# Ranking edges into slots: each partition's edges sorted by node, one-hots over a slice of the tiles, four columns to one 16-bit operation

## What is computed

```python
h = relu(layernorm(x))                        # x: (50000, 128) f32
agg = segment_sum(edge_attr, src, 50000)      # edge_attr: (25000, 128) f32
z = silu(concat([h, agg]) @ W1 + b1) @ W2 + b2   # W1 256x256, W2 256x128
z = (z - mean(z)) * rsqrt(var(z) + 1e-5) * gamma + beta
out = x + z + h
```

## Time and profile before

| | |
|---|---|
| median of 3 runs | 728.39 us (728.29 to 728.58) |
| the profiled execution | 728.61 us |
| its span, first to last instruction | 727.0 us |
| PE busy | 702.9 us (97%) |
| DVE busy | 710.3 us (98%) |
| ACT busy | 630.5 us (87%) |
| POOL busy | 475.7 us (65%) |
| mean granted TensorE clock | 0.991 |

### The profile page before, as it was taken

One profiled execution on the slowest core, in us unless ns is written; L12 is line 12 of the kernel. 1 busy time (PEld: TensorE's weight loads), 2 busy tenths in 40 slices (PEclk: granted clock), 3 DMA queues, 4 the chain that ended last, 5 costly groups with the idle time before them and its releaser, 6 DMA issues.

```text
span 727.0 us, 15386 instructions
## 1 busy us (share of the span) xinstructions
PE 702.9 (97%) x4554; PEld 589.8 (81%) x4554; DVE 710.3 (98%) x2275; ACT 630.5 (87%) x2034; POOL 475.7 (65%) x414
## 2 busy tenths in 40 slices
PE   7999998799999999999999999999999999999993
PEld 3555554689898989889898989898989898988993
DVE  8999998999999999999999999999999999999998
ACT  7999996679898989898888989898989898989883
POOL 3000006777777787777787777787777787877850
PEclk9999999989999999999999999999999999999998
DMA  5000000214233333333333423242424242422212
GB/s 214 2 1 1 1 0 16 54 55 137 94 126 104 117 110 112 116 107 119 100 123 97 134 86 136 84 139 81 139 81 138 81 138 83 139 77 78 73 49 83
DMA packets 28265, 65.89 MB, mean 91 GB/s; under 512 B 8473, under 2 KB 10028, under 8 KB 28180
## 3 DMA queue, kind: packets, MB, share of 16 engines
q1 hardware_dynamic: 15604, 51.90, 20.2%
q0 software_dynamic: 12576, 12.99, 7.4%
HBM read 52.05 MB, written 25.60 MB: 107 GB/s over the span
## 4 chain that ended last, share of the span: by engine, by line
DVE 63%; issue 19%; PE 13%; POOL 1%; DMA 1%; DVEq 0%; ACT 0%
DVE T L1034 14%; DVE lo L1022 10%; DVE stat L824 10%; DVE R L1004 8%; DVE R L1029 7%; PE y L658 4%; PE za L653 2%; PE pre L653 2%; PE za L646 2%; PE pre L646 2%; DVE R L1051 2%; POOL G L436 1%; DVE guess_off L877 1%; DVE mdd L860 1%; DVE var L863 1%
## 5 line engine op out<-in xcount | busy, mean ns | idle before, releaser
L436 POOL DMA_INDIRECT G<-in_edge_attr_dram,slot_edge x388 | 465.4, 1200 | 119.8 <-issue 90.2
L741 PEld LDWEIGHTS y<-w2c,S 128*128 128x128 f32 (+1 forms) x1556 | 188.3, 192 | 8.0
L741 PE MATMUL y<-w2c,S 128*128 128x128 f32 (+1 forms) x1556 | 189.3, 275 | 0.0
L539 ACT ACTIVATE H<-X,shift,rstd 128x128 f32<-128x128 f32 x392 | 161.9, 489 | 2.8 <-DVE shift L882 2.8
L716 PE MATMUL pre<-hi,w1h 128*128 128x512 f32 (+1 forms) x392 | 164.0, 418 | 0.0
L717 PE MATMUL pre<-hi,w1l 128*128 128x512 f32 (+1 forms) x392 | 154.8, 395 | 0.0
L556 ACT ACTIVATE S<-pre,b1c 128x512 f32<-128x512 f32 (+1 forms) x196 | 125.5, 701 | 4.9 <-PE pre L721 4.8
L721 PE MATMUL pre<-lo,w1h 128*128 128x512 f32 (+1 forms) x392 | 123.3, 396 | 0.1
L1022 DVE TENSOR_TENSOR lo<-za,hi 128x1024 fp32r<-128x1024 f32 (+1 forms) x98 | 119.2, 1217 | 2.6 <-ACT hi L549 2.6
L824 DVE BATCH_NORM_STATS2 stat<-X 128x6 f32<-128x128 f32 x392 | 106.8, 282 | 0.1
L702 PE MATMUL za<-HOT,G 128*128 128x128 f32 (+1 forms) x784 | 104.9, 277 | 1.0 <-DMA G<-in_edge_attr_dram,slot_edge 0.9
(11 more groups left out here) (154 smaller groups left out, 1045.8 us busy)
## 6 DMA issues: line engine op xcount, KB each, us to landing
X<-in_x_dram SPq DMA_DIRECT2D x48, 512.0 KB, 3.6
out_dram<-R SPq DMA_DIRECT2D x48, 512.0 KB, 2.7
G<-in_edge_attr_dram,slot_edge POOLq DMA_INDIRECT x388, 2.6
X<-in_x_dram SPq DMA_DIRECT2D x1, 424.0 KB
out_dram<-R SPq DMA_DIRECT2D x2, 192.0 KB
w1f<-in_L_gnn_W_dram SPq DMA_DIRECT2D x1, 256.0 KB, 2.8
w2f<-in_L_gnn_W_dram SPq DMA_DIRECT2D x1, 128.0 KB, 2.6
srci<-in_src_dram SPq DMA_DIRECT2D x1, 85.8 KB
```

The source lines that it names most:

```text
L436: nc.gpsimd.indirect_dma_start(G[b.j][:, t, :], None, source, bass.IndirectOffsetOnAxis(ap=slot_edge[:, bass.ds(b.number(TILES, t), 1)], a ...
L539: done = nc.scalar.activation(H0[b.j][:, t, :], X[b.xj][:, t, :], ACT.Relu, bias=shift[b.j][:, t:t + 1], scale=rstd[b.ring(POWERS_LAG)][:, ...
L741: done = nc.tensor.matmul(places[t][0:r], S[c][:, m, t * r:(t + 1) * r], w2c[:, m, :], start=False, stop=True, skip_group_check=True)
```

## The change

Each partition's 200 edges (EC is now 200: 125 full partitions, three empty ones) are sorted by node, descending, on DVE: `largest` takes the eight largest of 200 keys (MAX), `strike` overwrites them with -1 (MATCH_REPLACE). A key is node * 256 + column + 1, exact in fp32. Since column n then holds each partition's n-th largest node, its tiles lie in a window computed from n alone (`window`, common to four columns). One-hots, ranks and table matmuls run over that window only. `hot_tile`, `is_slot` and `hot_slot` are made for four columns by one operation each, with the column as the innermost index, all operands fp16; `copy_ranks` brings the ranks to fp16. ACT takes all ranks. The words of an edge are now its column with the low part of its node's row, and its partition with the high part, so `table_words`, `edge_fields`, `slot_tables` decode them differently. The test for the slow path now sums the free slots, so that it also notices an edge outside its window. Sorting, unpacking and the slots of three groups earlier are interleaved by hand in `group_step`.

```diff
-BATCH = 7
-UNROLL = 4 * BATCH
-LAG_TABLE = 2 * BATCH
+SORTED = 8
+UNROLL = 40
+LAG_SLOT = 3
+LAG_TABLE = 4 * STREAMS
+WINDOW_SPREAD = 4.0
+WINDOW_MARGIN = 10.0
...
+    def window(n):
+
+        middle = (n + 0.5) / EC
+        reach = WINDOW_SPREAD * math.sqrt(middle * (1.0 - middle) / EC) + WINDOW_MARGIN / EC
+        first = max(0.0, 1.0 - middle - reach) * nodes
+        final = min(1.0, 1.0 - middle + reach) * (nodes - 1)
+        return slice(int(first) // BLOCK * TILES, (int(final) // BLOCK + 1) * TILES)
...
+    SORTS = [slice(0, SORTED)] + [slice(n, n + 2 * SORTED) for n in range(SORTED, EC, 2 * SORTED)]
...
-            nc.gpsimd.iota(edge_no[:], [[1, EC]], base=0, channel_multiplier=EC)
-            done = nc.gpsimd.iota(iota_tile[:], [[1, NT]], base=0, channel_multiplier=0, **small_iota)
+            nc.gpsimd.iota(column_no[:], [[1, EC]], base=1, channel_multiplier=0)
+            nc.gpsimd.iota(own_row[:], [[1, 1]], base=0, channel_multiplier=1, **small_iota)
+            done = nc.gpsimd.iota(iota_tile[:], [[1, NT], [0, STREAMS]], base=0, channel_multiplier=0, **small_iota)
...
-                nc.scalar.activation(junk_rank[:, s, :], counts[s][:, 0:NT], ACT.Relu, bias=neg_big[:],
+                nc.scalar.activation(junk_rank[:, s, width(column)], counts[s][:, tiles_near(column)], ACT.Relu,
...
-                    nc.tensor.matmul(counts[column.ring(STREAMS)][:, 0:NT], before[:],
-                                     hot_tile[:, column.ring(UNROLL), :], **add).then_inc(counted, 1)
+                    nc.tensor.matmul(counts[column.ring(STREAMS)][:, tiles_near(column)], before[:],
+                                     hot_tile[:, place(column), width(column), column.ring(STREAMS)],
+                                     **add).then_inc(counted, 1)
...
-                                     hot_slot[:, late.ring(UNROLL)].rearrange("p w r -> p (w r)"),
-                                     hot_tile[:, late.ring(UNROLL), :], **add).then_inc(slot_free, 1)
+                                     hot_slot[:, place(late), :, :, late.ring(STREAMS)].rearrange("p w r -> p (w r)"),
+                                     hot_tile[:, place(late), width(late), late.ring(STREAMS)], **add).then_inc(slot_free, 1)
...
+            def largest(n):
+
+                dve.wait_ge(sort_step, 2 * n + 1)
+                nc.vector.max(out=top[:, n * SORTED:(n + 1) * SORTED], in_=keys[:]).then_inc(sort_step, 1)
+
+            def strike(n):
+
+                dve.wait_ge(sort_step, 2 * n + 2)
+                nc.vector.match_replace(out=keys[:], in_to_replace=top[:, n * SORTED:(n + 1) * SORTED],
+                                        in_values=keys[:], imm_value=-1.0).then_inc(sort_step, 1)
...
+            def group_step(g):
+                late = g.plus(-LAG_SLOT)
+                if late.exists(GROUPS):
+                    copy_ranks(late)
+                if g.exists(GROUPS):
+                    sort_first(g)
...
+                    dve.wait_ge(slot_free, g.number(STREAMS, STREAMS))
+                    columns = slice(g.number(STREAMS), g.number(STREAMS, STREAMS))
+                    nc.vector.tensor_tensor(out=hot_tile[:, g.ring(UNROLL // STREAMS), 0:w], in0=iota_tile[:, near],
+                                            in1=tile_of[:, columns].unsqueeze(1).to_broadcast([P, w, STREAMS]),
+                                            op=ALU.is_equal).then_inc(tile_hot, 1)
+                    sort_second(g)
+                if late.exists(GROUPS):
+                    is_slot_of(late)
+                if g.exists(GROUPS):
+                    sort_third(g)
+                if late.exists(GROUPS):
+                    hot_slot_of(late)
...
+                nc.vector.tensor_tensor(out=hot_slot[:, g.ring(UNROLL // STREAMS)],
+                                        in0=is_slot[:].unsqueeze(1).to_broadcast([P, 2, CAP, STREAMS]),
+                                        in1=word[:, :, columns].unsqueeze(2).to_broadcast([P, 2, CAP, STREAMS]),
+                                        op=ALU.mult).then_inc(slot_hot, 1)
```

More of the change, by code:

```diff
@@ L110, in gnn_layer @@
     NT = NB * TILES
-    EC = -(-edges // P)
+    EC = next(n for n in range(-(-edges // P), edges + 1) if edges % n == 0 and n % SORTED == 0)
     FULL = edges // EC
-    REST = edges - FULL * EC
     FIRST_BLOCKS = 3
@@ L117, in gnn_layer, with common @@
     LAST_SMALLS = 9
[L118 to L121, removed]
+    assert FULL % 16 and 16 < FULL < P and EC < 1 << COLUMN_BITS and nodes <= OUTSIDE < 1 << 16
+    assert EC % UNROLL == 0 and UNROLL % STREAMS == 0 and NT <= 512 and SORTED % STREAMS == 0
+    def window(n):
[4 more added lines that the diff above has]
+        return slice(int(first) // BLOCK * TILES, (int(final) // BLOCK + 1) * TILES)
+    GROUPS = EC // STREAMS
+    def common(g):
+        near = [window(n) for n in range(g * STREAMS, (g + 1) * STREAMS)]
+        return slice(min(w.start for w in near), max(w.stop for w in near))
+    WINDOWS = [common(g) for g in range(GROUPS)]
+    WIDEST = max(w.stop - w.start for w in WINDOWS)
+    SORTS = [slice(0, SORTED)] + [slice(n, n + 2 * SORTED) for n in range(SORTED, EC, 2 * SORTED)]
+    assert SORTS[-1].stop == EC
     GROUP = max(n for n in range(1, 129) if edges % n == 0)
@@ L276, in run_columns, with tiles_near, width, place @@
                 step(Item(n))
[L278 to L290, removed]
+        def tiles_near(column):
+            return WINDOWS[column.group(STREAMS)]
+        def width(column):
+            return slice(0, tiles_near(column).stop - tiles_near(column).start)
+        def place(column):
+            return column.ring(UNROLL) // STREAMS
         last = Block(NB - 1)
@@ L807, in _ @@
[L807 to L817 removed]
+            dve.wait_ge(src_loaded, 16 * 2)
@@ new lines, in sort_third, with copy_ranks @@
+            def sort_third(g):
+                ahead = sort_number(g) + 1
+                if sort_number(g) == 0 and sort_place(g) == 1:
+                    strike(2 * ahead)
+                    tile_fields(SORTS[ahead], ahead)
+                    tiles(SORTS[ahead], ahead)
+                elif sort_place(g) == 2 and ahead < len(SORTS):
+                    tiles(SORTS[ahead], ahead)
+            def copy_ranks(g):
+                dve.wait_ge(ranked, g.number(STREAMS, STREAMS))
+                columns = slice(g.number(STREAMS), g.number(STREAMS, STREAMS))
+                nc.vector.tensor_copy(rank16[:, columns], rank[:, columns]).then_inc(ranks_copied, 1)
@@ L941, in _ @@
+            largest(0)
+            strike(0)
+            as_integers(SORTS[0], 0)
+            tile_fields(SORTS[0], 0)
+            tiles(SORTS[0], 0)
+            for n in range(GROUPS + LAG_SLOT):
+                group_step(Item(n))
             dve.wait_ge(counts_copied, 1)
```

275 lines of the change are left out of this document (142 added, 133 removed).

## The result

The changed kernel takes **710.71 us**, median of 4 runs (710.52 to 711.05), against 728.34 us for the kernel before in the same session (728.23 to 728.58): a ratio of 0.9757, with an interval of 0.9745 to 0.9769. The forecast was 708.6 us, range 700 to 723, faster with 0.84. The sign and the range held; the time is 2.1 us above the forecast.

What follows compares the result with a forecast made beforehand. DVE was taken to bound the front stage after the change, narrowly over PE's upper price. Tables copied 21.3 us earlier plus 1.5 us of table arithmetic gave -19.8 us: 708.6 us, range 700 to 723.

Steps and rivals of the forecast that it cites:

- What bounds after: Front stage, ranking edges into slots: DVE stays the bound at 1.61 us per group of four columns, 80.6 us for 50.
- its signs: Front stage: hot_slot near 0.42 us, 160-tile hot_tile near 0.49, MAX near 0.36, first table copy at 87 to 90 us.
- PE well under: Sign for the front stage: DVE over 95% busy and PE well under that.
- the second rival: Front stage: PE becomes the bound through weight loads or stride, +18.4 us, 727 us, about no change; chance 0.10.
- The 16-bit price: DVE's three large operations per group, 1299 elements with 16-bit operands: 0.52 ns per element, 0.68 us.
- The first rival: DVE's 16-bit operations still run at one element per cycle: 33.8 us more, 742 us, slower; chance 0.12.
- Sorting: DVE, per four groups: two MAX 0.56, two MATCH_REPLACE 0.84, nine small operations 0.81; 2.21 us, 0.55 per group.
- PE after: Front-stage matmuls over windows: three per column at 0.17 to 0.37 us, 0.67 to 1.46 us per group, not the bound.
- ACT after: Front-stage rank sums over 128 elements start every 0.25 us: 1.0 us per group, not setting the pace.
- The head: Before the first hot_tile: iota_tile takes 1.46 us (0.46 to 1.84), first hot_tile at 6.9 us, 1.3 later than 5.57.
- The end: After the last group: three steps of 0.11 us, then 0.89 us kept to the words' copy; tables copied at 88.7 us.
- Table arithmetic: Extra decoding operations: +0.4 us over the first 24 columns, +1.1 in block 1, +1.5 in all.

Runs made afterwards that it cites:

- experiment 3: Changed kernel with hot_tile in pairs of columns, two interleaved instead of four, so a matmul reads every 4 bytes: 708.93 us, ratio 0.973.
- Experiment 1: Changed kernel with tile_of, ranks and words in fp32 again, so no large DVE operation has all operands in 16 bits: 741.22 us, ratio 1.0173.
- experiment 8: On the kernel with pairs, keys first and long iota runs, ACT writes ranks as fp16 and DVE's rank copy goes: 701.73 us, ratio 0.9633.
- Experiments 6: Two separate edits of the changed kernel: keys no longer wait for iota_tile, 709.62 us; tile and slot iotas written in long runs, 710.65 us.
- experiment 7: Changed kernel with pairs of columns, keys before iota_tile and long iota runs together: 704.42 us, ratio 0.9671.
- experiment 5: Changed kernel with hot_tile column by column, made by four one-column operations, so PE reads consecutive numbers: 719.91 us, ratio 0.9881.

## Why the prediction was right, and where it was off

**What bounds after: DVE, right for most of the stage.** DVE is 98% busy from 10 to 60 us and 95% over the whole stage. Its own pace, seen where PE isn't in the way (experiment 3), is 77.7 us, 1.55 a group; the prediction had 1.61 and 80.6. Of its signs, hot_slot, hot_tile and MAX came as named, and the table copy at 90.03 us is just outside its 87 to 90. "PE well under" failed: PE is 95% busy over the stage, and the sign of the second rival, DVE waiting for ranks while PE is full, shows from 60 us on.

**The 16-bit price, right.** It was taken as 0.52 ns per element, half of the two-tensor price. Experiment 1 measures the other half as 0.52, and hot_slot is 0.425 us, as named beforehand. 
The Trainium skill, page "VectorE: DVE Perf Modes", section "Why `tensor_tensor` can't do 2×_2P or 4×", puts two results a cycle as the limit of a two-tensor operation; no such operation measured here was quicker than 0.52 ns per element.

**The first rival's price, right.** It was put at 33.8 us for 16-bit operations at the old price, and 742 us. Experiment 1 makes them so: 741.22 us, and a stage 33.5 us over DVE's own pace (111.2 against 77.7). Against the changed kernel it is 30.6, because 2.9 us of that one are PE's.

**Sorting, sized a little too high.** The term was 2.21 us per four groups. MAX came out at the assumed 0.28. The match-replace with its load costs 0.34 or 0.35 instead of 0.42, the rank copy 0.07 instead of 0.09. The nine small operations, start to start from 53.52 to 59.96 us, sum to 0.80 us, as forecast: most cost 0.07 or 0.08, but one of the `word` operations 0.14 and the sum `tile_of` 0.11. That is 0.15 + 0.08 + 0.01 = 0.24 per four groups, 3.0 us in all, the 2.9 between 80.6 and 77.7. 
The Trainium skill, page "Vector Engine (DVE) Microarchitecture Reference", section 3.9, describes a match-replace as a load and one pass. The trace agrees: it shows MATCH_VALUE_LOAD and MATCH_REPLACE8, and the 0.36 that the prediction worked out from it lies close to the 0.34.

**PE after, mis-sized.** The step "at 0.165/392 a column the matmul streams 0.056 us" took the price of columns 2 bytes apart. At 8 bytes it is 0.90 ns a column, 0.144 us for 160: 3 x 4 x 0.144 = 1.73 us for a full-width group, more than the upper price of 1.46 and than DVE's 1.61. So the second rival, PE as the bound by a stride that costs, was real, though for 2.9 us instead of 18.4, since most of the time it is near DVE's own need. By chance this and the last term cancel: 80.6 forecast, 80.6 measured. The clock had no part in it: it was granted in full from 40 to 80 us.

**ACT after, mis-sized, without effect here.** "1.0 us per group" came from 128-wide sums of the block stage. The sums of ranks start 0.37 us apart at 160 tiles, 1.48 us a group (experiment 8), close under DVE's 1.55. Once DVE got quicker, ACT held it up in places.

**The head, mis-sized.** The step "0.85 ns each, with 1568 numbers 1.46 us" failed: 3.40 us. The bounds given (0.46 to 1.84) didn't hold it. The first hot_tile came 1.9 us late, 8.77 instead of 6.9, the largest single error that nothing cancelled. Experiments 6 and 7 show it to be recoverable.

**The end.** From the last hot_slot to the copy of the words it was 0.64 us, 0.25 less than kept. The three steps put at 0.3 us behind the 80.6 lie inside the measured stage. 1.9 - 0.3 - 0.25 give the 1.3 us by which the copy was late (90.03 instead of 88.7). Behind it 0.8 us more were lost, which no term had. The matmuls into slot order wait for two copies of words, DVE's and ACT's. Timelines of ACT and PE, the first two rows from the trace before, the last two from the changed kernel:

```profile
110.28 0.46 ACT L520 CAST words<-y 128x392 f16<-128x392 f32 x1
110.84 0.32 PE L672 MATMUL y<-words,ident 64*128 64x392 f16 x1 [0.84 <-DVE words L949]
```

```profile
90.77 0.46 ACT L535 CAST words<-y 128x392 f16<-128x392 f32 x1
91.33 0.48 PE L685 MATMUL y<-words,ident 64*128 64x392 f16 x1 [1.52 <-DVE words L1039]
```

ACT's copy started 0.24 us after DVE's before (110.04) and 0.74 after it now (90.03), since it stands behind ACT's sum over `total`, and PE starts 0.10 us after its end both times. That is 0.5 of the 0.8 us. In the trace before, DVE's copy had waited for PE's last tables, which gave ACT's chain its time. The other 0.3 us lie between PE's start and the first row that reads the result: 0.96 us (91.33 to 92.29) against 0.64 (110.84 to 111.48). The granted clock was 0.70 in 90 to 100 us, and the 392-wide matmul there takes 0.48 us against 0.32; PE had been idle for 1.52 us before it, and 0.84 in the trace before. That the lower clock costs the 0.3 us is read from the lengths; no run kept the clock up here.

**Table arithmetic.** Block 1 was put at +1.1 us and cost 1.1 (from 19.0 to 17.9 us of lead). The first 24 columns were put at +0.4; the lead went from 19.2 to 18.8 there, but was 19.0 again at block 1's `lo`. **The sum**: -20.0 + 0.8 + 0.2 + 1.1 = -17.9, and the span is 18.0 us shorter, where -19.8 was forecast. These 1.8 us are 1.3 at the copy and about 0.5 behind it. The rest of the 2.1 us is in the medians: that of before lies 0.2 us under its profiled execution, that of the changed kernel 0.2 us above its own (710.52).

**The change as a whole.** Either half alone loses: windows without 16-bit operations 741.22 us, 16-bit operations without windows 838.59, or 747.59 with pairs. The windows shrink PE's work and make room for the stride that comes with DVE's operation; with pairs they are needed all the same, since over 392 tiles, with PE and ACT both full, the stage takes 116.5 us against 103.6 before (5.57 to 109.15).

## What to carry to other kernels

A layout that makes one engine's operation cheap is read by another engine: price both before choosing it. Here two columns interleaved gave DVE the same price as four, and PE nearly its full rate. A constant built once at the head is part of the path if the first operation waits for the same semaphore; four times the numbers may cost more than seven times the time. When a forecast meets the time within 0.3%, check the terms all the same: here two errors of some 3 us cancelled, and the 6.3 us that experiment 7 gains lay in one of them and in the head.

## What the runs showed of the hardware that was not expected

- **The step of the moving operand.** At full granted clock a matmul column (fp16) took 0.42 ns at a step of 2 bytes (392 in 0.165 us), 0.45 at 4 bytes (160 in 0.072) and 0.90 at 8 bytes (160 in 0.144, 392 in 0.35).
  The Trainium skill, page "SBUF — State Buffer", section "Door 1: The DMA port swizzle (why `[64,N]` ≈ `[32,N]`)", has a note that two hits on a 16-byte line are enough for full bandwidth. A step of 8 bytes makes two hits a line, and the rate was halved; the measurement decides.
- **GpSimd's iota.** 392 numbers took 0.46 us, 784 in long runs 1.00, 784 in runs of two 4.38, 1568 in runs of four 3.40, and 1568 in long runs 3.61. No single price per number or run fits all of these; what sets it stays open.
- **DVE beside an iota.** A cast of eight numbers took 1.82 us beside the iota, to the iota's end, against 0.16 with no iota beside it (experiment 7), and 0.41 beside the shorter one in the changed kernel; MAX8 and match-replace took 0.37 and 0.35 beside it, as elsewhere.
- **The clock in the stage.** In 20 to 40 us the granted clock was 0.79 in experiment 5, 0.50 in experiment 1 and 1.00 in experiment 3, with PE waiting for DVE in all three. DVE was 98 to 99% busy in each, so the clock didn't set their pace.
